# Moving the scan's input term from a PSUM bank to SBUF, and dealing six PSUM banks instead of five to the matrix products

## The reference

```python
def step(h, inp):
    dtt, ut, bt, ct = inp
    dA = dtt[:, :, None] * A
    barA = jnp.exp(dA)
    inp_term = jnp.einsum('bdn,bn,bd->bn', dA, bt, ut)
    h = barA * h + inp_term[:, None, :]
    y = jnp.einsum('bdn,bn->bd', h, ct) + Dp * ut
    return (h, y)
```

## Time and profile before

| what | value |
|---|---|
| median of 3 runs | 2318.24 us (2313.72 to 2318.61) |
| the profiled execution's own time | 2323.44 us |
| its span, first to last instruction | 2321.7 us |
| PE busy | 2053.9 us (88%) |
| DVE busy | 2015.2 us (87%) |
| ACT busy | 1857.6 us (80%) |
| POOL busy | 1271.2 us (55%) |
| scans (line 1588) | 512, from 78.2 to 2152.5 us |
| mean granted TensorE clock | 0.962 of full |

### The profile page before, as it was taken

How to read it: one execution, slowest core, us unless ns; L and a number is a source line. 1 busy time by engine, 2 the same in 40 slices (tenths; PEclk the granted TensorE clock), 3 DMA queues, 4 the chain that set the end, 5 groups by cost and what they waited for, 6 DMA issues and landing times. The chain is left out here.

```text
span 2321.7 us, 40659 instructions
## 1 busy us (share of the span) xinstructions
PE 2053.9 (88%) x12844; PEld 1291.1 (56%) x12844; DVE 2015.2 (87%) x3843; ACT 1857.6 (80%) x3544; POOL 1271.2 (55%) x1837
## 2 busy tenths in 40 slices
PE   2558899998989989898999989899998989989997
PEld 0225556474655646465564646556464655647574
DVE  6898988979989898998989899898989889897845
ACT  4788888897978889797888979788797978867463
POOL 6224455655645565564556556465555546554754
PEclk8669999999999999999999999999999999999999
DMA  3452322323132131423213132322323232321000
GB/s 86 121 133 60 105 57 69 85 61 95 53 94 66 50 102 46 111 54 86 74 50 95 54 99 56 93 67 59 87 62 94 58 96 58 90 63 48 6 6 12
DMA packets 104450, 165.97 MB, mean 71 GB/s; under 512 B 15458, under 2 KB 34094, under 8 KB 104238
## 3 DMA queue, kind: packets, MB, share of 16 engines
q1 hardware_dynamic: 104238, 163.37, 26.2%
HBM read 146.55 MB, written 16.78 MB: 70 GB/s over the span
## 5 line engine op out<-in xcount | busy, mean ns | idle before, releaser
L1588 DVE TENSOR_TENSOR_SCAN scan_bufs<-scan_bufs,inp_bank 128x512 f32<-128x512 f32 x512 | 614.4, 1200 | 6.0 <-ACT scan_bufs L987 4.4
L1304 PE MATMUL bank<-w_gu,f_xqT 128*128 128x512 f32 x1024 | 489.1, 623 | 31.6 <-ACT f_xqT L1050 29.3
L981 ACT ACTIVATE scan_bufs<-scan_bufs,a_rows 128x512 f32<-128x512 f32 x512 | 368.9, 724 | 34.5 <-DMA scan_bufs<-dt_copy 34.2
L1319 PE MATMUL bank<-w_dn,f_hqT 128*128 128x256 f32 x1536 | 360.2, 385 | 11.2 <-ACT f_hqT L1050 9.2
L1598 DVE TENSOR_TENSOR scan_bufs<-scan_bufs,c_bank 128x512 f32<-128x512 f32 x512 | 344.0, 672 | 0.3
L1304 PEld LDWEIGHTS bank<-w_gu,f_xqT 128*128 128x128 f32 x1024 | 197.2, 199 | 255.6 <-issue 246.8
L1319 PEld LDWEIGHTS bank<-w_dn,f_hqT 128*128 128x128 f32 x1536 | 286.6, 191 | 80.1 <-issue 33.0
L898 POOL TENSOR_SCALAR_AFFINE_SELECT masked_scores<-masked_scores 128x512 f32<-128x512 f32 x256 | 172.4, 699 | 242.8 <-ACT masked_scores L1050 241.5
L876 POOL TENSOR_TENSOR f_h<-f_h,f_h_scale 128x704 f32<-128x704 f32 x128 | 185.7, 1451 | 180.5 <-DVE f_h L1468 180.5
L987 ACT ACTIVATE scan_bufs<-scan_bufs 128x1024 f32<-128x1024 f32 x256 | 271.6, 1061 | 1.0
L887 POOL TENSOR_TENSOR f_h<-f_h,f_h_lean 128x704 f32<-128x704 f32 x128 | 222.3, 1737 | 85.6 <-DVE f_h L1649 72.6
(11 more groups left out here) (198 smaller groups left out, 4393.9 us busy)
## 6 DMA issues: line engine op xcount, KB each, us to landing
scan_bufs<-dt_copy SPq DMA_DIRECT2D x512, 256.0 KB, 4.1
xp<-L_attn_a_x SPq DMA_DIRECT2D x16, 512.0 KB, 4.1
dt_copy<-dt SPq DMA_DIRECT2D x32, 256.0 KB, 3.6
out<-x SPq DMA_DIRECT2D x64, 128.0 KB, 3.4
w_attn<-L_attn_b_W_attn SPq DMA_DIRECT2D x1, 768.0 KB, 5.2
masked_scores<-L_ffn_w_gate SPq DMA_DIRECT2D x1, 704.0 KB
masked_scores<-L_ffn_w_up SPq DMA_DIRECT2D x1, 704.0 KB
f_h<-L_ffn_w_down SPq DMA_DIRECT2D x2, 352.0 KB, 10.8
```

The lines of the kernel that those rows point to most:

```text
L981: nc.scalar.activation(half, half, ACT.Exp, scale=a_rows[:, c, at:at + 1]).then_inc(root_ready, 1)
L1304: last = nc.tensor.matmul(to[:, :], f.xqT[:, k, :], w_gu[:, k, g, lo:hi], start=(k == 0), stop=(k == DH - 1))
L1319: last = nc.tensor.matmul(to[:, 0:D], f.hqT[:, k, :], w_dn[:, k, :], start=(k == 0), stop=(k == FK - 1))
L1588: nc.vector.tensor_tensor_scan(half, half, inp[:, :], 0.0, ALU.mult, ALU.add)\
```

## The change

The input term becomes an SBUF tensor of 128 x 512 floats (2 KB in each partition), and the bank that it held goes to the pool. No instruction, no wait and no place in any engine's order is added or removed; the numbers of the banks that `Banks` deals out change throughout, since it now deals six.

```diff
-        b_rep = sb("b_rep", [P, T])
+        b_rep, inp = sb("b_rep", [P, T]), sb("inp", [P, T])
...
-        acc_y, c_rep, inp = bank("acc_y"), bank("c_bank"), bank("inp_bank")
-        banks = [bank(f"bank{j}") for j in range(5)]
+        acc_y, c_rep = bank("acc_y"), bank("c_bank")
+        banks = [bank(f"bank{j}") for j in range(6)]
         filled = [sem(f"bank{j}_filled") for j in range(len(banks))]
         drained = [sem(f"bank{j}_drained") for j in range(len(banks))]
         uses = Banks(len(banks))
```

## The result

The changed kernel takes 2523.45 us, against 2318.1 us for the kernel before in the same comparison: a ratio of 1.088 (95% interval 1.0855 to 1.0907), 205 us more. The 2523.45 is the median of four executions, one of which took 7839.59 us; the ratio and its interval are of the other three. The profiled execution took 2516.88 us, with a span of 2515.2.

What follows compares the result with a forecast made beforehand. The prediction took chains through several engines to set the period, with PE 91% and DVE 90% busy. Its sum was 2323.4 + 108 + 41 - 8 = 2464, less 5 giving 2460 us, range 2335 to 2595.

Steps and rivals of the forecast that it cites:

- The mechanism: Scans with two SBUF inputs and POOL's SBUF reads exclude each other; longest scan over 2 us, mean near 1.4.
- Scans that wait for POOL: On DVE, some 222 of 512 scans, starting at random times, meet a POOL instruction and wait: 108 us, ends nothing and 195.
- POOL instructions that wait: On POOL, instructions starting inside a scan wait, 258 us in all, 16% of it on the path: 41 us.
- The sixth bank: On PE, one more pool bank ends bank waits of at most 24.9 us; a third taken, -8 us.
- The scan's own duration: On DVE, an undisturbed scan takes the same with both inputs in SBUF: no difference, ends -4 to +1 us.
- The reserve takes it: Rival: DVE's 214 us of idle time takes the scans' 108 us of waiting; 2334 to 2359 us, chance 0.12.
- All of POOL's lateness on the path: Rival: all 258 us of POOL's waiting for scans reaches the end; 2684 us, chance 0.06.
- The scan does not contend: Rival: POOL goes on beside scans with two SBUF inputs and the extra bank pays; 2293 us or lower, chance 0.08.
- It does nothing: Rival: no contention, and PE's bank waits are only replaced by waits for data; 2318 us, chance 0.04.

Runs made afterwards that it cites:

- late_pool: The kernel before plus, in front of 436 POOL instructions, a memset sized to each one's excess in the changed kernel's profile: 2380.28 us, ratio 1.029.
- five_banks: The changed kernel with five pool banks instead of six, the input term still in SBUF: 2522.31 us, ratio 1.088.
- six_banks_alone: The changed kernel, six pool banks, its scans reading C's bank instead of the input term, each batch's first also waiting for C: 2316.74 us, ratio 0.9993.
- odd_batches: The kernel before, five pool banks, with the input term written to and read from SBUF in the eight odd batches only: 2420.76 us, ratio 1.046.
- late_both: The kernel before plus DVE reductions before late scans and POOL memsets before late POOL instructions, sized to their excesses: 2510.41 us, ratio 1.085.

## Why the prediction was right, and where it was off

**The mechanism** held in each of its signs. The longest scan, forecast over 2 us, is 3.02; the scans' mean, forecast near 1.4 us, is 1.55; POOL's busy time, forecast up by some 260 us, rose by 301; the longest of line 887 went from 2173 to 2617 ns; the bank waits of the earlier trace rows went and the waits for POOL grew. That DVE and POOL exclude each other when both of DVE's inputs lie in SBUF is what the Trainium skill says in "SBUF — State Buffer", section "Who interferes with whom"; the scan, which no row of the kernel before could show, behaves as the other forms do. It does so throughout: of the 255 scans that start in the changed kernel while an instruction of POOL's eight large groups is under way, nine in ten end 1.07 to 1.08 us after that instruction, wherever in it they started. But not every instruction of POOL that reads SBUF holds a scan up for all its length:

```profile
1478.97 1.02 POOL L910 TENSOR_TENSOR p_rstd<-p_var,minus_half 128x4 f32<-128x4 f32 x1
...
1479.40 1.22 DVE L1588 TENSOR_TENSOR_SCAN scan_bufs<-scan_bufs,inp 128x512 f32<-128x512 f32 x1
```

This power of four columns has 0.59 us to go when the scan starts, and the scan takes its usual time. So do all of the scans that start in such narrow instructions of POOL (lines 849 to 859, 906 and 910). None of them is in the eight groups that the forecast counted.

**The size** was 142 us in the forecast and is 205. The terms, one by one:

*Scans that wait for POOL* were mis-sized most, by the step that let scans start at random times. The excesses over 0.15 us are 176 us in 216 scans, 0.81 us each; the working had 222 scans at 108 / 222 = 0.49. That 222 and 216 lie close is luck, for they do not count the same: 255 scans start while an instruction of the eight groups is under way, and the 216 are those of them with more than a little of it to go. These 255 find 0.84 us to go on the mean, where random starts gave 141 / 222 = 0.64: they meet longer instructions (1.42 us on the mean, where a random start meets 1.27), and they meet them a little before half-way, on the mean after 42%. The starts are not random because the order of each engine is fixed and the two engines release each other: 95 of these 255 instructions of POOL had waited for a step of DVE, as at 1144.21 us, and the scan starts 0.46 us after POOL at the median. All this could be read before the change. In the trace of the kernel before, 255 scans already start while one of the eight groups is under way, with 0.85 us to go on the mean, 217 us together; less 0.15 us each this is 178 us, and the scans' busy time rose by 179. The upper bound of that term, 195 us by the 0.88 us of the earlier trace rows, was nearer. That it all shows at the end was too much: 78% do, so the term gave 129 us where the sum had 108.

*POOL instructions that wait* gave 66 us, not 41. The lateness was 301 us where the sum had 258, and the share on the path 23%, where I had counted 16% of takers that already waited. In the changed kernel 155 of 640 takers wait, 24%, and in late_pool, where POOL alone was made late, 136. So lateness makes new takers wait, and the count taken before it was too low. That the share of takers is near the share of the lateness that reached the end is not shown to be more than chance.

*The sixth bank* gave nothing, not -8. With the data late the bank's waits were there and cost nothing (five_banks against the change); without the lateness the 25 us did not show either (six_banks_alone). The forecast took PE's semaphore waits to be unchanged; there are 70 more, and the second of these runs, which has them too, is no slower. Nor were the 24.9 us the most that a bank could give: they are the three largest kinds of such waits, and smaller ones, as line 1313 for the bank of `hqT` with 3.2 us, come on top.

*The scan's own duration* did not change: 1151 ns at the least in both kernels. The figures of the Trainium skill's "VectorE: DVE Perf Modes", by which each scan would be 65 ns shorter, do not show.

With 129 - 108 = 21, 66 - 41 = 25, the bank's 8 and the 9 us that the rebuilt lateness leaves out, the sum is the 63 us between forecast and result. The 9 us are a remainder, not a measured term.

**The rivals.** *The reserve takes it* fails on odd_batches: half the dose costs half the loss, so there is no free first part. *All of POOL's lateness on the path* fails on late_pool: 23%. *The scan does not contend* and *It does nothing* fail on the scan's tail.

What remains open: the last 9 us, within which lie the excesses under 0.15 us that were left out and DVE's other instructions; and why evenly spread DVE time cost 53% and the scans' waits 78%. Their lengths differ (0.24 us more of busy time for every scan against 0.81 on 216), and so do their places (behind the scan, in front of it); no run separates the two.

## What to carry to other kernels

Before moving an operand of DVE, count its inputs in SBUF: a second one makes POOL's reads of SBUF wait for the instruction, and the instruction for POOL's wide reads, and the sign for it in this kernel is a line whose longest duration is a multiple of its median. An input in PSUM is worth a bank when DVE and POOL both work hard: here the bank held by the input term was worth 205 us, and the same bank in the pool of products nothing. Price such a wait from the trace before the change, by the instructions that already start inside each other and how much of the first is left, not by random starts: here the count gives 178 us and random starts 108, and 179 was measured.

## What the runs showed of the hardware that was not expected

**POOL's writes do not hold DVE up.** In late_pool a memset of POOL runs into a rounding of DVE with both inputs in SBUF (lines 1555 and 1560 are lines 1463 and 1468 of the kernel before, line 968 is line 876). DVE's timeline, then POOL's:

```profile
1235.01 0.87 DVE L1555 SCALAR_TENSOR_TENSOR f_h_lean<-f_h_abs,f_h 128x704 f32<-128x704 bf16 x1
...
1235.91 1.19 DVE L1560 SCALAR_TENSOR_TENSOR f_h<-f_h_abs,f_h_lean 128x704 f32<-128x704 bf16 x1
```

```profile
1234.73 0.79 POOL L934 MEMSET pool_ring<- 128x822 f32 x1
1235.48 0.87 POOL L968 TENSOR_TENSOR f_x<-f_x,f_x_inv 128x256 f32<-128x256 f32 x1
```

The memset has 0.51 us to go when line 1555 starts, and that takes 0.87 us, no more than undisturbed (885 ns in the median before). The product that follows on POOL, which reads SBUF, starts inside line 1555 and takes 0.87 us in place of its usual 0.62; and line 1560, started while that product runs, takes 1.19 in place of 0.89. The case is not a single one: of the 35 roundings of late_pool (lines 1555 and 1560) that start with over 0.2 us of a memset to go, none is over its usual duration by more than 0.01 us; 133 that start with as much of another instruction of POOL to go take 0.45 us more on the mean. The Trainium skill says this too, in "SBUF — State Buffer", section "Who interferes with whom": a GpSimd instruction that only writes SBUF does not contend. The trace agrees.

**TensorE's granted clock fell with the lateness.** In the stretch of the scans it was 0.97 of 2.4 GHz on the mean before and 0.94 after, with PE busy 91% before and 85% after. It stood at 1.2 GHz for 135 us of that stretch before and for 263 us after, and at 2.4 GHz for the rest. One such fall: PE waited 3.13 us for `y_tok` (line 1408, up to 1158.05 us), and from 1158.4 to 1165.2 us the clock was 1.2 GHz, though PE was busy 6.62 of those 6.80 us. PE's busy time in the stretch rose by 39 us for the same products, of which the second trace holds a few less (11687 and 11823 records). late_both, which has the lateness and no scan with two SBUF inputs, shows the same 0.94, and six_banks_alone 0.97. So the fall comes with the lateness and not with the place as such. That PE's longer waits bring it about is likely but was not tested alone, and what it costs at the end was not measured; whatever it is, it is a part of the 205 us and of late_both's 196.
